# A four-layer Macaron block on one core: separate rings for B and C, gates in two transfers, other turns, and every second pair of states added on GpSimd

## What is computed

```
x = x + 0.5 * ffn0(norm(x))        # norm, ternary 128->512, gelu, norm, ternary 512->128
x = x + attn0(norm(x))             # scan over 16 states, gate gelu(z), 128->128
x = x + 0.5 * ffn0(norm(x))
x = x + 0.5 * moe(norm(x))         # sigmoid encoder, 8 experts, top-2 gates, decoder
x = x + mamba(norm(x))             # conv, silu, then the selective scan:
    h[t] = exp(delta[t]*A) * h[t-1] + delta[t]*u[t]*B[t]      (256 channels x 16 states,
    y[t] = sum over the 16 states of h[t] * C[t]               restarted every 32 rows)
    out  = (y * silu(res)) @ W_out
x = x + 0.5 * moe(norm(x))
```

## Time and profile before

| | us |
|---|---|
| median of 3 runs (lowest, highest) | 1186.02 (1185.41, 1189.14) |
| the profiled execution, its own time | 1187.36 |
| its span in the trace | 1185.6 |
| granted TensorE clock, mean | 0.904 of full |

### The profile page before, as it was taken

How to read it: one execution, slowest core, us unless ns; L and a number is a source line. 1 busy time by engine, 2 the same in 40 slices (tenths; PEclk the granted TensorE clock), 3 DMA queues, 4 the chain that set the end, 5 groups by cost and what they waited for, 6 DMA issues and landing times.

```text
span 1185.6 us, 11091 instructions
## 1 busy us (share of the span) xinstructions
PE 943.9 (80%) x3350; PEld 438.6 (37%) x3350; DVE 734.6 (62%) x1653; ACT 674.6 (57%) x1073; POOL 595.0 (50%) x476
## 2 busy tenths in 40 slices
PE   6456986798789978997899789997998679867645
PEld 4333343343344334433444443343443333422311
DVE  3213216873789559774988298738884688289711
ACT  3344575676567667657675877475775444433211
POOL 2121236552765565565656465727653666266412
PEclk9767798899899999999899999998899789988956
DMA  3002007350626064425523363425360635155220
GB/s 127 10 0 81 1 3 252 112 177 19 240 107 250 1 223 153 178 71 164 212 94 155 109 224 140 152 50 210 112 244 11 249 142 214 55 196 197 96 80 9
DMA packets 40747, 151.79 MB, mean 128 GB/s; under 512 B 2544, under 2 KB 10864, under 8 KB 38640
## 3 DMA queue, kind: packets, MB, share of 16 engines
q1 hardware_dynamic: 40688, 151.09, 36.1%
HBM read 148.20 MB, written 2.88 MB: 127 GB/s over the span
## 4 chain that ended last, share of the span: by engine, by line
PE 41%; DVE 24%; ACT 14%; DMA 8%; POOL 7%; issue 7%; SPq 0%; DVEq 0%; POOLq 0%; ACTq 0%
DVE dA L975 11%; PE yp L1482 8%; DMA bcast<-held 5%; ACT L125 4%; PE pp L1360 4%; PE mp L1440 4%; POOL dbu L706 3%; PE mp L1425 3%; PE fp L1246 3%; DVE hs L980 3%; PE pp L1226 3%; PE fp L1262 2%; PE mp L1226 2%; PE mp L1450 2%; PE pp L1330 2%
## 5 line engine op out<-in xcount | busy, mean ns | idle before, releaser
L706 POOL TENSOR_TENSOR dbu<-du,bcast 128x1024 f32<-128x1024 f32 x128 | 301.2, 2354 | 142.6 <-DMA bcast<-held 82.2
L975 DVE TENSOR_TENSOR_SCAN dA<-dA,dbu 128x512 f32<-128x512 f32 x256 | 312.7, 1221 | 82.6 <-POOL dbu L706 48.3
L1482 PE MATMUL yp<-hs,ident 128*128 128x512 f32 x512 | 282.2, 660 | 59.2 <-DVE hs L980 59.0
L1204 ACT ACTIVATE dA<-delta,pr 128x512 f32<-128x512 f32 x256 | 173.7, 685 | 119.9 <-DVE hs L980 119.2
L980 DVE TENSOR_TENSOR hs<-dA,bcast 128x512 f32<-128x512 f32 x256 | 177.0, 691 | 9.3 <-PE yp L1482 0.6
L1482 PEld LDWEIGHTS yp<-hs,ident 128*128 128x128 f32 x512 | 92.3, 205 | 188.5 <-DVE hs L980 118.9
L125 ACT ACT_TABLE_LOAD x109 | 139.8, 1283 | 18.9 <-POOL delta L629 17.0
L656 POOL TENSOR_TENSOR he<-he,gsp 128x512 f32<-128x512 f32 x64 | 81.0, 1270 | 61.3 <-ACT he L1171 37.0
L1425 PE MATMUL mp<-cont,ex_ 64*128 64x512 f32 x128 | 77.4, 686 | 20.6 <-DVE he L938 19.5
L1429 PE MATMUL mp<-cont,ex_ 64*128 64x512 f32 x128 | 77.8, 690 | 1.7 <-ACT he L1171 1.6
L1262 PE MATMUL fp<-w,hT 128*128 128x129 f32 x512 | 66.6, 280 | 12.3 <-ACT sq L1021 5.7
(11 more groups left out here) (214 smaller groups left out, 1417.1 us busy)
## 6 DMA issues: line engine op xcount, KB each, us to landing
bcast<-held SPq DMA_DIRECT2D x104, 1024.0 KB, 5.8
gsp<-gheld SPq DMA_DIRECT2D x16, 2048.0 KB, 9.6
xin<-L_attn_x SPq DMA_DIRECT2D x8, 256.0 KB, 5.2
out<-xb SPq DMA_DIRECT2D x8, 256.0 KB, 2.4
ex_<-c_ex SPq DMA_DIRECT2D x1, 985.0 KB, 7.1
bcast<-c_ps SPq DMA_DIRECT2D x1, 768.0 KB, 8.5
pr<-c_pr SPq DMA_DIRECT2D x1, 567.0 KB, 9.4
held<-dbc SPq DMA_DIRECT2D x8, 64.0 KB, 1.6
```

Source lines behind the costliest of these rows:

```text
L706: pool.tensor_tensor(out=dbu[:, j % 2, :].rearrange("p (r t) -> p r t", r=2), in0=d, in1=b_n, op=ALU.mult).then_inc(dbu_r.sem, 1)
L975: dve.tensor_tensor_scan(out=dA[:, half], data0=dA[:, half], data1=dbu[:, j % 2, half], initial=0.0, op0=ALU.mult, op1=ALU.add).then_inc(h ...
L1204: act.activation(out=dA[:, r * SEQ:(r + 1) * SEQ], in_=delta[:, i % 2, c, :], func=ACT.Exp, scale=mA[:, c, 2 * k + r:2 * k + r + 1]).then_ ...
L1482: pe.matmul(yp[:, :], lhsT=ident[:, :], rhs=hs[:, j % 2, r * SEQ:(r + 1) * SEQ], start=(s % PAIRS == 0 and r == 0), stop=(s % PAIRS == PAI ...
```

## The change

There are five edits. **One:** `bcast` becomes two rings, `b_row` and `c_row`, of three slots each, with a 0.5 MB load for each. A B slot is free when GpSimd has multiplied, a C slot when VectorE has. On SP the load of C j stands behind that of B j. `dbu` waits for B alone, the product `hs` for C. SP issues 208 loads of rows instead of 104. **Two:** the gates are loaded in two transfers of 1 MB, experts 0 to 3 and 4 to 7, each with a semaphore. **Three:** in steps with odd s, 64 of 128, GpSimd adds the second half of `hs` to the first, in place, once both are written, and TensorE sums one row in place of two: 24 products a sequence for 32. On GpSimd the add of step j-1 stands behind `dbu` of step j, with a `yield` between, and other threads' steps may lie there. **Four:** moef i+3 comes ahead of moeb i, and mpre i+2 ahead of the front of moeb i, both in `P_TURNS` and `M_TURNS`. **Five:** all five strings of `ORDER` are new. TensorE's sums of |w| at the start are both issued before the products with w1, the second into a column of `dA`.

```diff
-M_TURNS = [("moef", 0), ("moef", 1), ("moef", 2)]
-for _i in range(BATCH):
-    M_TURNS.append(("moeb", _i))
-    if _i + 3 < BATCH:
-        M_TURNS.append(("moef", _i + 3))
...
+FRONTS = "f0 m0 f1 m1 f2 o0 m2 f3 b0 o1 m3 f4 b1 o2 m4 f5 b2 o3 m5 f6 b3 o4 m6 f7 b4 o5 m7 b5 o6 b6 o7 b7".split()
...
     "SP":
-        "AGAGBBBBBBABBGBGBBBBBBBBBBABBBGBGBBGBGBBBDBBBBBABBGBGGGBBBBBBDBBBBABBBGBGBBGBGBBBBBBBBABBGDBGGGBBBBB"
...
+        "AGAGGBBBBBBBBBBBBBBBBAGBGGBBBBBBBBBBBBBBBBBBBBBBBBBBBAGGGBBBBBBBBBBBBBBBBBBBBBBBBBBBAGGGGBGGBBBBBBBB"
...
     "PE":
-        "EPFPEFFFFFFFFFFFFFFFFFFFFFFFFFPFPFFPFFPFEPFFPPFFEEFEFEEPFEFEFFFFFFFPPPFPFPFFPPFFFPFFSPSPSSSPSPSSEPFS"
...
+        "PFFEEFFFFPFFFFFFFFFFFFFFFFFFFFPFPFFPFFPFEPFFPPPFEFEEFEEFEEFFFFFFPFPFFPPPFPFPFPFFFFSFSFPSPPSPPESSSPSF"
...
+ADDED = [_s for _s in range(STEPS) if _s % 2 == 1]
+SUMS = [1 if _s in ADDED else 2 for _s in range(STEPS)]
...
+B_SLOTS, C_SLOTS = 3, 3
...
+class Rows:
+    def __init__(self, slots):
+        self.slots, self.slot, self.load, self.after = slots, {}, {}, {}
+        free_after, loads = [-1] * slots, [0] * slots
+        for j in range(BATCH * STEPS):
+            i, s = divmod(j, STEPS)
+            twin = i * STEPS + 2 * PAIRS - 1 - s
+            if PAIRS <= s < PAIRS + slots:
+                self.slot[j], self.load[j] = self.slot[twin], self.load[twin]
+                continue
+            at = min(range(slots), key=lambda x: free_after[x])
+            loads[at] += 1
+            self.slot[j], self.load[j], self.after[j] = at, loads[at], free_after[at]
+            free_after[at] = twin if PAIRS - slots <= s < PAIRS else j
...
-        bcast = sb("bcast", [P, SLOTS, 2, 2 * SEQ])
+        b_row = sb("b_row", [P, B_SLOTS, 2 * SEQ])
+        c_row = sb("c_row", [P, C_SLOTS, 2 * SEQ])
...
-                        if LOADED_AFTER[j] >= 0:
-                            sp.wait_ge(dbu_r.sem, LOADED_AFTER[j] + 1)
-                            sp.wait_ge(hc_r.sem, 2 * (LOADED_AFTER[j] + 1))
...
+                        if j in B_ROWS.after:
+                            yield True
...
+                            if B_ROWS.after[j] >= 0:
+                                sp.wait_ge(dbu_r.sem, B_ROWS.after[j] + 1)
...
+                        if j in C_ROWS.after:
+                            yield True
+                            if C_ROWS.after[j] >= 0:
+                                sp.wait_ge(hc_r.sem, 2 * (C_ROWS.after[j] + 1))
...
-                    if m >= 1:
-                        sp.wait_ge(her_e.sem, her_e.at(m - 1, EP))
-                        sp.wait_ge(her_o.sem, her_o.at(m - 1, EP))
-                    src = gheld[m % 2, :, :].rearrange("(a e) t -> a e t", a=1)
-                    sp.dma_start(gsp[:, :, :], src.broadcast_to([P, EXPERTS, SEQ])).then_inc(g_in.sem, 16)
+                    for part in range(2):
+                        yield True
+                        some = slice(part * EP, (part + 1) * EP)
...
+                            sp.wait_ge(her_e.sem, her_e.at(m - 1, EP // 2 * (part + 1)))
+                            sp.wait_ge(her_o.sem, her_o.at(m - 1, EP // 2 * (part + 1)))
+                        src = gheld[m % 2, some, :].rearrange("(a e) t -> a e t", a=1)
+                        sp.dma_start(gsp[:, some, :], src.broadcast_to([P, EP, SEQ])
+                                     ).then_inc(g_in[part].sem, 16)
...
-                    if k == 0:
-                        pool.wait_ge(g_in.sem, g_in.at(m, 16))
+                    if k % 2 == 0:
+                        pool.wait_ge(g_in[k // 2].sem, g_in[k // 2].at(m, 16))
...
+            def add_pair(j):
+                pool.wait_ge(hc_r.sem, 2 * (j + 1))
+                pool.tensor_tensor(out=hs[:, j % 2, 0:SEQ], in0=hs[:, j % 2, 0:SEQ], in1=hs[:, j % 2, SEQ:2 * SEQ],
+                                   op=ALU.add).then_inc(pair_r.sem, 1)
...
-                        pool.wait_ge(bc_in[SLOT_OF[j]], 16 * LOAD_NO[j])
+                        pool.wait_ge(b_in[B_ROWS.slot[j]], 16 * B_ROWS.load[j])
...
+                        if j >= 1 and (s - 1) % STEPS in ADDED:
+                            yield True
+                            add_pair(j - 1)
+                yield True
+                add_pair(j)
...
+                            if r == 0:
+                                dve.wait_ge(c_in[C_ROWS.slot[j]], 16 * C_ROWS.load[j])
                             if j >= 2:
-                                dve.wait_ge(sum_ps.sem, h - 3)
+                                dve.wait_ge(sum_ps.sem,
+                                            sums_before(j - 2) + (1 if (s - 2) % STEPS in ADDED else r + 1))
...
-                        for r in range(2):
+                        for r in range(SUMS[s]):
                             yield True
-                            pe.wait_ge(hc_r.sem, 2 * j + r + 1)
+                            if s in ADDED:
+                                pe.wait_ge(pair_r.sem, adds_before(j) + 1)
+                            else:
+                                pe.wait_ge(hc_r.sem, 2 * j + r + 1)
```

More of the change, by code:

```diff
@@ L30 @@
 AX = mybir.AxisListType.X
-M_TURNS = [("moef", 0), ("moef", 1), ("moef", 2)]
-for _i in range(BATCH):
-    M_TURNS.append(("moeb", _i))
-    if _i + 3 < BATCH:
-        M_TURNS.append(("moef", _i + 3))
-P_TURNS = [("front", M_TURNS.index(("moef", 0))), ("mpre", 0), ("front", M_TURNS.index(("moef", 1))), ("mpre", 1),
-           ("front", M_TURNS.index(("moef", 2)))]
-for _i in range(BATCH):
-    P_TURNS += [("mout", _i), ("front", M_TURNS.index(("moeb", _i)))]
-    if _i + 2 < BATCH:
-        P_TURNS.append(("mpre", _i + 2))
-    if _i + 3 < BATCH:
-        P_TURNS.append(("front", M_TURNS.index(("moef", _i + 3))))
+FRONTS = "f0 m0 f1 m1 f2 o0 m2 f3 b0 o1 m3 f4 b1 o2 m4 f5 b2 o3 m5 f6 b3 o4 m6 f7 b4 o5 m7 b5 o6 b6 o7 b7".split()
@@ L47 @@
+M_TURNS = [({"f": "moef", "b": "moeb"}[_t[0]], int(_t[1])) for _t in FRONTS if _t[0] in "fb"]
+P_TURNS = [({"m": "mpre", "o": "mout"}[_t[0]], int(_t[1])) if _t[0] in "mo" else
+           ("front", M_TURNS.index(({"f": "moef", "b": "moeb"}[_t[0]], int(_t[1])))) for _t in FRONTS]
 ORDER = {
     "SP":
-        "AGAGBBBBBBABBGBGBBBBBBBBBBABBBGBGBBGBGBBBDBBBBBABBGBGGGBBBBBBDBBBBABBBGBGBBGBGBBBBBBBBABBGDBGGGBBBBB"
-        "BDBBBBBBBGBGBBGBGBBDBBBBBBBBGBGBGBGBBBBBBBBBBBGBGBBBBDBDGGD",
+        "AGAGGBBBBBBBBBBBBBBBBAGBGGBBBBBBBBBBBBBBBBBBBBBBBBBBBAGGGBBBBBBBBBBBBBBBBBBBBBBBBBBBAGGGGBGGBBBBBBBB"
+        "BDBBBBBBBBBBBBABBBBGGGBGGGBBBBBBBBBBBBBBBBDBBBBBBBBBBAGGGBBGGGBBBBBBBBBBBBBBBBBDBBBBBBBBGGBGBGGGBBBB"
+        "BBBBBBBBBBBBBDBBBBBBBBBGGGGBGGBBBBBBBBBDBBBBBBBBBBBBBBBBGBGGBBBBBBBBBGGBDGGGGDD",
@@ L381, in build @@
         g_out = signal("g_out", 16)
-        g_in = signal("g_in", 16)
+        g_in = [signal(f"g_in{k}", 16) for k in range(2)]
         dn = Norm("d_", 2)
@@ L431, in build @@
         yg = sb("yg", [P, IC, SEQ])
-        bc_in = [sem(f"bc_in{k}") for k in range(SLOTS)]
+        b_in = [sem(f"b_in{k}") for k in range(B_SLOTS)]
+        c_in = [sem(f"c_in{k}") for k in range(C_SLOTS)]
         dA_r = signal("dA_r", STEPS)
@@ L488, in spread @@
                     if i >= 2:
-                        for s in range(SLOTS):
-                            used = sum(SLOT_OF[j] == s and j in LOADED_AFTER for j in range((i - 1) * STEPS))
-                            sp.wait_ge(bc_in[s], 16 * used)
+                        for rows, arrived in ((B_ROWS, b_in), (C_ROWS, c_in)):
+                            for at in range(rows.slots):
+                                sp.wait_ge(arrived[at], 16 * rows.loads_before(at, (i - 1) * STEPS))
                     sp.dma_start(held[i % 2, :, :, :].rearrange("s n t -> (s n) t"), dbc[64:96, :]
```

128 lines of the change are left out of this document (61 added, 67 removed).

## The result

| | before | after |
|---|---|---|
| median of the runs, us | 1185.72 | 1166.93 |
| lowest, highest | 1184.28, 1189.14 | 1164.11, 1170.55 |
| ratio to before, 95% interval | | 0.9839 [0.9802, 0.9876] |
| span of the profiled execution | 1185.6 | 1166.7 |
| granted TensorE clock, mean | 0.904 | 0.883 |

The account below looks back on a forecast made before the run. The bound was taken to change with the stage: TensorE in the middle, scans with VectorE fullest late. Terms -4-38-22-15-3+14+14=-54 took 1187.4 to 1133, or 1132 on the median's scale; range 1097 to 1186.

Parts of the forecast that it names:

- 1 start: Before the first scan, TensorE's P set-up comes earlier, so the first transposes start sooner: -4 us, bounds -6 and 0.
- step 2: TensorE's sums with 64 products fewer, counting most in the middle: -38 us, gain bounded by 24 and 70 us.
- step 3: New turns bring the next sequence's du earlier, closing gaps between the last scans: -22 us, bounds 0 and -35.
- rival D: The turns fail: du is still late before the scans and last adds wait for it; 1160 us, chance 0.10.
- Step 4: Separate rings for B and C let B land sooner, cutting GpSimd's wait for loads: -15 us, bounds 0 and -60.
- Step 6: On ScalarE, 30 more table loads at 0.44 us each on the chain: +14 us, bounds 0 and +38.
- Step 7: 64 adds on GpSimd, costing by their place in its queue: +14 us, bounds +5 and +83.
- (a): On GpSimd, add and next dbu just fit VectorE's pair time, with other threads' steps sometimes between: 4 us.
- rival C: GpSimd's add and dbu set the pace of odd pairs, making scans late: slower, 1210 us, chance 0.15.
- (b): At steps 7 and 15, yg on VectorE waits for an add besides the sum, 16 times: 10 us.
- (c): A sequence's last GpSimd add stands behind the next one's first dbu: free as long as du is early.
- Rival B: Most of the gain is eaten, as in-order engines near 70% hold each other up: 1175 us, chance 0.15.

Follow-up runs that it names:

- searched letters: Letters of all five strings replaced by a search's: the changed kernel so reordered took 1118.68 us, without its adds 1112.02, the kernel before 1163.29.

## Why the prediction was wrong

| step | predicted | with the letters as given | with searched letters |
|---|---|---|---|
| 1 start | -4 | first transposes at 13.3 us as said, the layer's first output `fx` at 35.1 for 38.2: -3 | |
| 2 64 products fewer | -38 | +9 in before, -14 in after | +1 to +3 |
| 3 other turns | -22 | about 0, what is left of +1.5 for steps 1, 3, 5 and 6 | -25 or more |
| 4 two rings | -15 | -12 in before, -23 in the new order | -22 |
| 5 gates in two | -3 | the bare load at the end 4.58 us for 7.05 | |
| 6 30 more table loads | +14 | +7 | |
| 7 64 adds | +14 | +17 | about +3 |

With the letters as given, a chain of kernels leads from before to after: start, turns, gates and table loads +1.5, the rings -23, 64 products fewer -14, the adds +17, in all -19. The prediction had -15, -15, -38 and +14 for the same four. What it lacks is 24 us in step 2 and some 22 in step 3; the rings and the table loads give 8 and 7 of these back.

**Step 2 is the step that failed most.** The prediction took 0.6 us for each of the 64 products, between the 0.37 of the chain and the full 1.10. Its reason was TensorE's 87% in the middle. But a busy share is not an amount of work: with fewer products the clock falls, those that are left take longer (an instruction 660 to 713 ns in before, 645 to 665 in after), and the share stays where it was, 86% in before's middle at 0.93 of the clock for 88% at 0.99 (the stretch from 425 us). That the share would stay is what the prediction wanted to see; it didn't take it as a warning. The last sentence of the prediction names this as a way to be wrong; it had no price in the sum, and the lower bound of the term, 24 us of gain, shut it out. A bound below nothing was needed: nothing in the rows excluded a loss.

**Step 3 had the right mechanism and the wrong ledger.** The gaps closed, and scan follows upon scan as counted. I had written that the work in the gaps does not vanish, and took 13 us off for it. What I did not do is look at the letters of ScalarE and TensorE, where that work now lies between exponentials of the running scan (10.5 us at one place, against a gap of 18 closed) and ahead of its last sum (seven waits, 46 us without any add). Nor was the count right for GpSimd. With fitted letters turns and gates give 28 to 30 us, more than the 22 and 3 of the prediction. So the edit is good, and the given strings spend what it brings; which of their waits spend it isn't shown one by one. That this is rival D's result (the turns give nothing) came by another way than D's: `du` isn't late, the scans are slow.

**Step 4** was right in size, and its reason too, though "bounds 0 to -60" was wide. In the new order the rings are worth more (-23); why isn't shown. **Step 6:** the price of a load on the time is 0.23 us, by what falls away with all of them; the prediction's 0.44 came from the chain, which says who was last, not what would be last next. The Trainium skill, "ScalarE: Activation LUTs", "What ACT_TABLE_LOAD costs", gives 2.66 us a switch, the load with a drain, and by that the prediction worked out +29 for the 30 loads. Measured are +7, and the rows show no drain: a load that starts at 1004.98 and takes 1.28 is followed by an activation at 1006.27.

**Step 7** came out at its size, +17 for +14, but not by the waits counted; that the numbers agree is in part luck. (a) GpSimd isn't late for the scan: VectorE's wait for `dbu`, 48.3 us before, is 2.5 now; rival C did not happen. (b) and (c): the adds lengthen the wait at `yg` by 20 us, from 44.3 to 64.4. I had (c) as free; putting the last add early takes 18 us off that wait, but gained nothing, so what makes up the 17 stays open. And the larger part of the wait at `yg`, 44 us for 20.2 before, has nothing to do with the adds.

**Rival B,** "a late letter on one holds up the others", describes the outcome best, with 0.15 given to it. The searched kernels show it directly: nearly the same instructions, 48 us apart.

## What to carry to other kernels

When every engine is in order and none is full, price an edit by the order in which each queue takes its steps, on all five queues, not by the busy share of one; and after an edit fit the order again before judging it: the turns were worth nothing with one set of letters and nearly 30 us with another. Work taken from TensorE was no gain by itself where the clock fell with its load, as in these kernels: bound such a term below nothing. A wait that is removed is worth what the next wait in the same queue leaves of it: for the last add, nothing. And before a wait is put down to an edit, look whether it is there without the edit.

## What the chip did that I had not expected

- Taking 64 float32 products (7% of TensorE's busy time) out lowered the mean granted clock in all three kernels: 0.905 to 0.879, 0.910 to 0.894, 0.927 to 0.900 (means over the runs). Their effect on the time was +9, -14 and +3 us. Less work taken from other threads, 46 us in P and 33 in F, lowered it from 0.904 to 0.888 and 0.890.
- 64 products by zeros, 71 us of them, brought it back to 0.904, and the kernel was 7 us faster with them than without.
- 108 table loads of 1.283 us, 140 us of ScalarE's time, cost 25 us of the kernel's.
- From a stretch of 3.3 us in which TensorE was idle, and over one of 6.0 us, the clock was at 1.2 GHz for 23 us. With both filled it stayed at 2.4 GHz.
